# A recurrent two-tower network over 128 steps: path work less far ahead, the two column groups nearly a turn apart

## What is computed

```python
def _tower(x, w_in, b_in, blocks):          # _leaky(x) = where(x >= 0, x, 0.2 * x)
    h = _leaky(x @ w_in + b_in)
    for w1, b1, w2, b2 in blocks:           # two blocks, 128 x 128 each
        h = _leaky(_leaky(h @ w1 + b1) @ w2 + b2 + h)
    return h

def step(prev_delta, xk):
    fk, k = xk
    d = jnp.where(k == 0, fk[:, DELTA_IDX], prev_delta)
    fk = fk.at[:, DELTA_IDX].set(d)
    fe = _tower(fk[:, :4], fw_in, fb_in, flat_blocks)
    pe = _tower(fk[:, 4:], pw_in, pb_in, path_blocks)
    h = _leaky(jnp.concatenate([fe, pe], axis=-1) @ cw1 + cb1)
    delta = jax.nn.sigmoid(h @ cw2 + cb2)[:, 0]
    return (delta, delta)
```

## Time and profile before

| | |
|---|---|
| Median of 3 runs | 1250.41 us (1250.08 to 1253.89) |
| The profiled execution | 1254.54 us, its span 1252.7 us |
| PE busy | 1247.0 us, 6028 passes |
| PE weight loads busy | 1063.5 us |
| ACT busy | 931.0 us |
| DVE busy | 890.9 us |
| POOL busy | 11.8 us |
| DMA | 24.50 MB, 20 GB/s in the mean |

### The profile page before, as it was taken

One profiled execution on the slowest core, in us unless ns is written; L12 is line 12 of the kernel. 1 busy time (PEld: TensorE's weight loads), 2 busy tenths in 40 slices (PEclk: granted clock), 3 DMA queues, 4 the chain that ended last, 5 costly groups with the idle time before them and its releaser, 6 DMA issues.

```text
span 1252.7 us, 19624 instructions
## 1 busy us (share of the span) xinstructions
PE 1247.0 (100%) x6028; PEld 1063.5 (85%) x6028; DVE 890.9 (71%) x1950; ACT 931.0 (74%) x2049; POOL 11.8 (1%) x28
## 2 busy tenths in 40 slices
PE   9999999999999999999999999999999999999998
PEld 6888888888888888888888888888888888888886
DVE  3777777767777777777777777777777777777775
ACT  3777777777777777777777777777777777777776
POOL 1000000000000000000000000000000000000000
PEclk9999999999999999999999999999999999999999
DMA  2000000000000000001000000000000000000000
GB/s 75 30 10 31 13 10 30 13 30 10 24 20 11 29 13 24 17 10 33 11 23 19 12 30 10 30 13 11 29 14 29 10 21 22 11 23 12 13 4 1
DMA packets 14881, 24.50 MB, mean 20 GB/s; under 512 B 1983, under 2 KB 8214, under 8 KB 14782
## 3 DMA queue, kind: packets, MB, share of 16 engines
q1 hardware_dynamic: 13982, 22.33, 5.5%
q10 hardware_dynamic: 720, 0.66, 0.2%
q0 software_dynamic: 80, 0.26, 0.1%
HBM read 16.67 MB, written 6.55 MB: 19 GB/s over the span
## 4 chain that ended last, share of the span: by engine, by line
PE 98%; DMA 0%; ACT 0%; DVE 0%; issue 0%; ACTq 0%; DVEq 0%
PE ps_path L540 36%; PE ps_flat L540 18%; PE ps_res L543 18%; PE ps_head L670 9%; PE ps_head L665 9%; PE ps_head L683 2%; PE ps_head L678 2%; PE ps_path L570 2%; PE ps_flat L627 2%; DMA cb_col<-cb 0%; PE ps_path L565 0%; DVE f_t L448 0%; ACT delta L313 0%; DVE head_lo L482 0%; PE ps_flat L622 0%
## 5 line engine op out<-in xcount | busy, mean ns | idle before, releaser
L256 ACT ACTIVATE f_mid<-ps_flat,columns_sb 128x256 f32<-128x256 f32 x512 | 242.6, 474 | 161.9 <-PE ps_flat L540 155.5
L543 PE MATMUL ps_res<-f_mid,hidden_w 128*128 128x256 f32 x1024 | 306.1, 381 | 0.2
L540 PE MATMUL ps_path<-p_mid,hidden_w 128*128 128x256 f32 x1024 | 304.5, 380 | 0.0
L256 ACT ACTIVATE f_res<-ps_res 128x256 f32<-128x256 f32 x512 | 196.1, 384 | 62.4 <-PE ps_res L543 62.4
L540 PEld LDWEIGHTS ps_path<-p_mid,hidden_w 128*128 128x128 f32 x1024 | 190.9, 190 | 31.1 <-ACT p_mid L256 0.2
L543 PEld LDWEIGHTS ps_res<-f_mid,hidden_w 128*128 128x128 f32 x1024 | 168.6, 189 | 55.4 <-ACT f_mid L256 1.8
L414 DVE SCALAR_TENSOR_TENSOR p_sum<-ps_path,columns_sb,p_in 128x512 f32<-128x512 f32 x128 | 96.1, 751 | 126.9 <-PE ps_path L540 126.9
L256 ACT ACTIVATE p_mid<-ps_path,columns_sb 128x512 f32<-128x512 f32 x256 | 176.1, 688 | 6.4 <-PE ps_path L540 6.4
L476 DVE CAST head_hi<-head 128x256 fp32r<-128x256 f32 x256 | 75.3, 294 | 128.8 <-ACT head L256 128.7
L448 DVE SCALAR_TENSOR_TENSOR f_t<-delta,columns_sb,ps_flat 128x256 f32<-128x256 f32 x256 | 123.1, 481 | 50.0 <-ACT delta L313 48.9
L256 ACT ACTIVATE head<-ps_head,cb_scaled 128x256 f32<-128x256 f32 x256 | 121.2, 474 | 45.7 <-PE ps_head L670 39.6
(11 more groups left out here) (49 smaller groups left out, 1454.9 us busy)
## 6 DMA issues: line engine op xcount, KB each, us to landing
x_in<-x_hi SPq DMA_DIRECT2D x127, 48.0 KB
x_in<-x_lo SPq DMA_DIRECT2D x127, 48.0 KB
chunk_x<-x SPq DMA_DIRECT2D x16, 192.0 KB, 2.4
x_hi<-chunk_hi SPq DMA_DIRECT2D x16, 192.0 KB, 1.9
x_lo<-chunk_lo SPq DMA_DIRECT2D x16, 192.0 KB, 2.0
out<-delta SPq DMA_DIRECT2D x128, 2.0 KB
hidden_w<-hidden ACTq DMA_DIRECT2D x1, 384.0 KB, 5.7
hidden_w<-hidden ACTq DMA_DIRECT2D x1, 256.0 KB, 3.0
```

What stands on the lines that cost most here:

```text
L256: return act.activation(dst, src, ACT.Prelu, bias=bias, alpha=NEG)
L540: return pe.matmul(dst, weight[w_name], src, start=True, stop=True)
L543: return pe.matmul(dst, weight[w_name], src, start=False, stop=True, skip_group_check=True)
```

## The change

path_2b, the leaky function of the path's second sum, moves from DVE to ACT. The body of every engine is written anew and runs for k = 1 to 128. In body k the path work is now that of steps k (second half of path_2b), k + 1 and k + 2. Group 0 starts its step at the head of the body, and group 1 starts the same step about a third of the turn later and ends it (output_high, output_low, delta_out, head_high, head_low of k - 1) at the head of the next body. The openings are new lists: on DVE the input weights are split ahead of chunk 0, which now comes behind flat_delta and flat_in of both groups, and split_chunk(1) now stands ahead of path_2b_sum(0). In the lists of the openings only the new order is shown.

```diff
@@ -153,7 +153,7 @@
             return 0 <= k < STEPS
 
         def bodies(eng, body):
-            for k in range(FIRST_BODY, STEPS):
+            for k in range(FIRST_BODY, STEPS + 1):
                 body(k)
 
         @block.sync
@@ -276,6 +276,12 @@
                     act.wait_ge(s_p2a_mm, k + 1)
                     leaky(p_mid2[:, :], ps_path2[:, :], column["pr2_b1"]).then_inc(s_p2a_h, 1)
 
+            def path_2b(k):
+                par = k % 2
+                if exists(k):
+                    act.wait_ge(s_p2b_t, k + 1)
+                    leaky(p_res2[par][:, :], p_sum2[:, :]).then_inc(s_p2b_h, 1)
+
             def flat_1a(k, g):
                 if exists(k):
                     act.wait_ge(s_f1a_mm[g], k + 1)
@@ -315,49 +321,45 @@
 
             def body(k):
                 flat_1a(k, 0)
+                delta_out(k - 1, 1)
+                flat_1b(k, 0)
+                path_2b(k)
+                flat_2a(k, 0)
+                flat_1a(k, 1)
+                flat_2b(k, 0)
                 flat_1b(k, 1)
-                flat_1b(k, 0)
+                path_1b(k + 1)
+                head_out(k, 0)
                 flat_2a(k, 1)
-                flat_2a(k, 0)
+                path_in(k + 2)
                 flat_2b(k, 1)
-                path_1b(k + 2)
-                flat_2b(k, 0)
+                delta_out(k, 0)
+                path_2a(k + 1)
                 head_out(k, 1)
-                head_out(k, 0)
-                path_in(k + 3)
-                delta_out(k, 1)
-                path_2a(k + 2)
-                delta_out(k, 0)
-                path_1a(k + 3)
-                flat_1a(k + 1, 1)
+                path_1a(k + 2)
 
...
             path_in(0)
             path_1a(0)
             flat_1a(0, 0)
+            path_1b(0)
+            flat_1b(0, 0)
+            path_in(1)
             flat_1a(0, 1)
+            path_2a(0)
+            path_1a(1)
+            path_2b(0)
+            flat_2a(0, 0)
+            flat_2b(0, 0)
+            path_1b(1)
             flat_1b(0, 1)
+            head_out(0, 0)
             flat_2a(0, 1)
             path_in(2)
             flat_2b(0, 1)
+            delta_out(0, 0)
             path_2a(1)
             head_out(0, 1)
+            path_1a(2)
 
             bodies(act, body)
 
@@ -429,12 +431,6 @@
                         dve.wait_ge(s_p2b_h, k)
                     add(p_sum2[:, :], ps_path2[:, :], column["pr2_b2"], p_res1[par][:, :]).then_inc(s_p2b_t, 1)
 
-            def path_2b(k):
-                par = k % 2
-                if exists(k):
-                    dve.wait_ge(s_p2b_t, k + 1)
-                    leaky(p_res2[par][:, :], p_sum2[:, :]).then_inc(s_p2b_h, 1)
-
             def flat_delta(k, g):
                 par = k % 2
                 if exists(k):
@@ -490,46 +486,37 @@
             def body(k):
                 flat_delta(k, 0)
                 flat_in(k, 0)
+                head_high(k - 1, 1)
+                head_low(k - 1, 1)
+                flat_1b_old(k, 0)
+                path_2b_sum(k)
+                flat_delta(k, 1)
+                flat_in(k, 1)
+                flat_2b_old(k, 0)
                 flat_1b_old(k, 1)
-                flat_1b_old(k, 0)
-                path_1b_sum(k + 2)
+                path_1b_sum(k + 1)
                 flat_2b_old(k, 1)
-                flat_2b_old(k, 0)
-                path_2b_sum(k + 1)
-                path_2b(k + 1)
-                split_next_chunk(k)
-                head_high(k, 1)
-                head_low(k, 1)
                 head_high(k, 0)
                 head_low(k, 0)
-                flat_delta(k + 1, 1)
-                flat_in(k + 1, 1)
-
...
+                split_next_chunk(k)
+
             split_input_weights()
+            flat_delta(0, 1)
+            flat_in(0, 1)
             flat_delta(0, 0)
             flat_in(0, 0)
+            split_first_chunk()
+            flat_1b_old(0, 1)
             flat_1b_old(0, 0)
             path_1b_sum(0)
             flat_2b_old(0, 0)
+            split_chunk(1)
+            path_2b_sum(0)
             split_output_weights()
             path_1b_sum(1)
             head_high(0, 0)
+            flat_2b_old(0, 1)
             head_low(0, 0)
 
             bodies(dve, body)
 
@@ -685,32 +672,32 @@
 
             def body(k):
                 flat_1a(k, 0)
-                flat_1b(k, 1)
-                path_1b(k + 2, 1)
+                output_high(k - 1, 1)
+                path_2b(k, 1)
+                output_low(k - 1, 1)
+                flat_x(k, 1)
                 flat_1b(k, 0)
-                flat_2a(k, 1)
-                path_2b(k + 1, 1)
+                path_1b(k + 1, 0)
+                path_1b(k + 1, 1)
                 flat_2a(k, 0)
-                flat_2b(k, 1)
+                flat_1a(k, 1)
                 combine_path(k, 0)
                 flat_2b(k, 0)
+                flat_1b(k, 1)
+                combine_path(k, 1)
+                combine_flat(k, 0)
+                flat_2a(k, 1)
+                flat_x(k + 1, 0)
+                path_in(k + 2)
+                path_2a(k + 1, 0)
+                output_high(k, 0)
+                flat_2b(k, 1)
+                output_low(k, 0)
+                path_2a(k + 1, 1)
+                path_1a(k + 2, 0)
                 combine_flat(k, 1)
-                flat_x(k + 1, 0)
-                path_in(k + 3)
-                combine_flat(k, 0)
-                flat_x(k + 1, 1)
-                path_2a(k + 2, 0)
-                output_high(k, 1)
-                path_2a(k + 2, 1)
-                output_low(k, 1)
-                output_high(k, 0)
-                path_1a(k + 3, 0)
-                output_low(k, 0)
-                path_1a(k + 3, 1)
-                combine_path(k + 1, 1)
-                path_2b(k + 2, 0)
-                flat_1a(k + 1, 1)
-                path_1b(k + 3, 0)
+                path_1a(k + 2, 1)
+                path_2b(k + 1, 0)
 
             def output_weight_rows():
                 pe.wait_ge(s_one_row, 1)
@@ -724,58 +711,43 @@
...
                 if i >= WARM_UP - GROUPS:
                     opening.then_inc(s_res_open[i % GROUPS], 1)
             path_in(0)
+            flat_x(0, 1)
             flat_x(0, 0)
             path_1a(0, 0)
             path_1a(0, 1)
+            output_weight_rows()
             flat_1a(0, 0)
             path_1b(0, 0)
             path_1b(0, 1)
             flat_1a(0, 1)
             flat_1b(0, 0)
             path_in(1)
             path_2a(0, 0)
+            path_2a(0, 1)
             path_1a(1, 0)
             path_1a(1, 1)
+            path_2b(0, 0)
+            path_2b(0, 1)
             flat_2a(0, 0)
             path_1b(1, 0)
             path_1b(1, 1)
             flat_2b(0, 0)
+            combine_path(0, 0)
+            flat_1b(0, 1)
+            combine_flat(0, 0)
+            combine_path(0, 1)
+            flat_2a(0, 1)
+            path_2a(1, 0)
+            flat_x(1, 0)
             path_in(2)
+            output_high(0, 0)
             flat_2b(0, 1)
+            output_low(0, 0)
+            path_2a(1, 1)
             path_1a(2, 0)
+            combine_flat(0, 1)
             path_1a(2, 1)
             path_2b(1, 0)
 
             bodies(pe, body)
```

More of the change, by code:

```diff
@@ L336, in _ @@
             flat_1a(0, 0)
+            path_1b(0)
+            flat_1b(0, 0)
+            path_in(1)
             flat_1a(0, 1)
-            path_1b(0)
-            path_in(1)
+            path_2a(0)
[4 more added lines that the diff above has]
+            path_1b(1)
             flat_1b(0, 1)
-            flat_1b(0, 0)
-            path_1a(1)
-            path_2a(0)
+            head_out(0, 0)
             flat_2a(0, 1)
-            flat_2a(0, 0)
-            path_1b(1)
             path_in(2)
-            flat_2b(0, 0)
             flat_2b(0, 1)
-            path_1a(2)
+            delta_out(0, 0)
             path_2a(1)
             head_out(0, 1)
[L353 to L360, removed]
+            path_1a(2)
             bodies(act, body)
@@ L492, in body @@
                 flat_in(k, 0)
+                head_high(k - 1, 1)
[5 more added lines that the diff above has]
+                flat_2b_old(k, 0)
                 flat_1b_old(k, 1)
-                flat_1b_old(k, 0)
-                path_1b_sum(k + 2)
+                path_1b_sum(k + 1)
                 flat_2b_old(k, 1)
-                flat_2b_old(k, 0)
-                path_2b_sum(k + 1)
-                path_2b(k + 1)
-                split_next_chunk(k)
-                head_high(k, 1)
-                head_low(k, 1)
                 head_high(k, 0)
                 head_low(k, 0)
-                flat_delta(k + 1, 1)
-                flat_in(k + 1, 1)
-            split_first_chunk()
+                split_next_chunk(k)
             split_input_weights()
+            flat_delta(0, 1)
+            flat_in(0, 1)
             flat_delta(0, 0)
             flat_in(0, 0)
-            flat_delta(0, 1)
+            split_first_chunk()
```

(51 more changed lines are left out.)

## The result

The changed kernel takes 1272.93 us in the median of four runs (1271.49 to 1273.27) against 1252.15 for the kernel before beside it (1250.08 to 1253.97): a ratio of 1.0163, 95% interval 1.0145 to 1.0181. It is slower, by less than 2% but clear of the scatter: the slowest of these executions of before took 1253.97 us, the fastest of after 1271.49. The 1252.15 lies between two heaps of times of the kernel before (experiment 7), and none of the four took it. The profiled execution of after is 1272.63 us with a span of 1270.8, 18.1 above the one of before (1254.54, span 1252.7).

A forecast was written before the change was run, and what follows sets the result against it. It took PE's own work as the bound, so the middle could only gain holes; 9.5 (steps) + 4.8 (opening) + 3.2 (end) = +17.5 us on the 1250.4 median gave 1267.9, range 1256 to 1276.

The forecast's parts named there:

- opening: Up to flat_1a(1, 0): PE waits 7.3 us for late chunk 1, then runs at half clock; +4.8 us (+1.9 to +8.1).
- 125 steps: Steady steps run whole: 0.076 us a step of new PE holes, +9.5 us (bounds +6.2 and +12.5).
- end: From step 126 to the span's end, group 1 running behind group 0: +3.2 us.
- the residual decides: PE's flat_1b(k, 0) waits for DVE's flat_1b_old(k, 0): 0.070 us short, the larger of two shortfalls there.
- f_mid's hop: From flat_1a(k, 0) to flat_1b(k, 0): 0.789 us of products between, 0.833 wanted, 0.044 short.
- output_high(k, 0): On PE, waiting for the head: can start at 6.76 against its slot at 6.754, 0.006 us a step.
- The rival that the weight load doesn't wait for data: PE's weight loads: each hop 0.11 us shorter, both shortfalls gone, step stays 9.58, 1258.4 us; chance 10%.
- the one of more holes: Steady step: waits taken as met by 0.03 or less are not; 0.1 us a step more, 1280 us; chance 7%.
- lost to the clock: After the opening's hole, PE passes run at half speed for 5.9 us, losing 2.9 us.
- That the later group pays for it: End of the kernel: group 1's later finish pays for the opening's 5.4 us less work ahead of flat_1a(1, 0).
- The move of path_2b: Leaky function moved from DVE (0.69 us) to ACT (0.62), wanted by 3.2, ending at 2.8: costed at nothing.
- The step that was off is the last one: Forecast median: before's median, 1250.41, 4.1 us below its profiled execution, plus 17.5 gives 1267.9.

The follow-up runs named there:

- experiment 7: Kernel before with output_weight_rows on PE moved ahead of flat_1a(0, 0) in the opening; 1250.91 us median of 12 against 1251.02, ratio 0.9996.
- experiment 3: Changed kernel without head_low of group 1, without the bias of flat_1a in group 0, then without both; 1270.73, 1271.94 and 1267.6 us.
- experiment 1: Changed kernel with split_chunk(1) on DVE moved from the opening to the end of body 1; 1262.41 us, ratio to before 1.009.
- experiment 4: Changed kernel with DVE's split of chunk 0 back at the head of its opening list; 1271.43 us in one execution.
- experiment 5: Changed kernel with 36, then 46, unread bf16 products on PE filling the hole ahead of flat_2b(0, 0); 1272.3 and 1269.77 us.
- both cuts: Changed kernel without head_low of group 1 and without the bias of flat_1a in group 0; 1267.6 us, period 9.600.
- experiment 6: Changed kernel with path_2b put back from ACT on DVE, behind path_2b_sum; 1355.98 us in one execution, period 10.32.
- experiment 8: Changed kernel with split_chunk(1) at the end of body 1 and flat_1b_old(k, 0) between head_high and head_low on DVE; 1259.3 us, ratio to before 1.0053.
- experiment 2: Changed kernel with flat_1b_old(k, 0) ahead of head_high and head_low of (k - 1, 1) on DVE; 1282.79 us, ratio 1.0251.
- 36 products: Changed kernel with 36 unread bf16 products on PE between path_1b(1) and flat_2b(0, 0); 1272.3 us in one execution.
- 46 products: Changed kernel with 46 unread bf16 products on PE between path_1b(1) and flat_2b(0, 0); 1269.77 us in one execution.

## Why the prediction was right, and where it was off

The forecast was 17.5 us more, 1272.0 for the profiled execution and 1267.9 for the median. Measured were 18.1 more and 1272.63 for the one, 1272.93 for the other; by the two medians of four the change is 20.8. By the terms of the sum, from flat_1a(1, 0), flat_1a(126, 0) and the end of the span in the two profiles:

| term | forecast | measured | from |
|---|---|---|---|
| opening | +4.8 | +3.6 | 39.72 against 36.10 |
| 125 steps | +9.5 | +10.9 | 1208.8 against 1197.9 |
| end | +3.2 | +3.6 | 22.3 against 18.7 |

- **The steady step** went by its steps: the residual decides, f_mid's hop is second (experiment 3), output_high(k, 0) is the third. The chain 0.50, 0.40, 0.34, 0.48, 0.12 is in the rows of after to 0.01 as it was priced from the earlier trace rows. Forecast 0.076, measured 0.081 by the medians: 10.1 us. The other 0.8 are odd steps, below. The rival that the weight load doesn't wait for data fell: it starts 0.12 behind the residual, and the period is 9.66. So did the one of more holes.
- **The opening** went by its mechanism: chunk 0 later, chunk 1 at 28.2 (forecast 28.8), DVE idle for it 12.3 us, a hole ended at 31.1 (31.8), 2.4 us lost to the clock (2.9) (experiments 1, 4 and 5). These two make the 1.2 us between forecast and measurement: the transfer came 0.6 sooner than counted, and half speed lasted from 31.1 to about 35.8, not for 5.9 us. The 5.9 had been borrowed from the start, the nearest row there was, so that it came out near is partly luck. Mis-sized too is where the hole begins: 20.9 and not 24.5, 10.2 us and not 7.3, as the clock rose before 16 us in this execution. It did no harm and no good: the hole ends by the transfer.
- **The end**: step 126 took 9.50 as forecast, the last one and what follows 12.8 for 12.57. delta ended at 1268.67 + 0.47 = 1269.14, 11.15 behind flat_1a(127, 0) (forecast 10.97), and the span ended 1.7 later (1.6). That the later group pays for it is the prediction's account; no run tested it.
- **The move of path_2b** cost at most 0.018 us a step (experiment 3, both cuts), where it was put at nothing; without it the new order takes 10.32 (experiment 6).
- **The step that was off is the last one**, from the profiled execution to the median. I took the 4.1 us between the two for something that the kernel after would have as well, and subtracted it. By experiment 7 it is the early rise of the clock in the lower heap. The profile of after has the early rise already (20 passes for 16 to 21), and its hole ends by the transfer, at 31.1, whatever PE ran at before. So an early rise is spent in the hole, and the four executions of after make one heap, 1271.5 to 1273.3. A second reason isn't excluded: all eleven profiles of kernels in the new order have the early rise, and the four executions of experiment 8, where the hole is only 0.62 us, lie within 2.1 us. Perhaps the new opening never has the late one. Against the lower heap the change costs 22 us, against the upper one 18. The rows for it were there: three runs at 1250.1, 1250.4 and 1253.9, and a half-speed stretch up to 23.5 whose end decides 4 us.

## What to carry to other kernels

When PE has no hole, a new order can only be judged by laying every wait on a grid of the hops measured where PE really does wait; shortfalls of 0.04 and 0.07 us showed up to about a hundredth, 125 times over. An instruction whose data come late must not be queued ahead of one on the chain, least of all in an opening: moved behind, the same split of chunk 1 gave back 10.5 us. When a profile and the median differ, find what makes the difference before carrying it over to the kernel after: here it was an early clock, which the kernel after could gain nothing more from. And when an instruction is put forward in a tight queue, work out the new time of the one that it displaces (experiment 2).

## What the runs showed that was not expected

- The level that PE ran at in the first microseconds is not in the granted clock of most profiles: before and the kernel of experiment 7 both read 1.00 for 16 to 21 us, with 10 and 25 passes. In two of the thirteen (experiments 1 and 2: 0.50 and 0.56 for 10 to 15) it is. The fall after the hole is there, as 0.50. Count passes.
- A hole of 3.1 us, behind a PE that had been dense, was followed by passes 0.43 apart until 34.6 us (36 products). With no hole (46 products) and with one of 0.62 us (experiment 1) full speed stayed.
- On DVE the distance from start to start depends on what is read. Behind f_in (128x256) the residual of the other group starts 0.34 us later, and the residual that reads this f_in 0.46 later (before, and experiment 2). f_in starts 0.51 behind the f_t that it reads, head_lo 0.40 behind the shorter head_hi.
- A few steps in each profile are 0.1 to 0.4 us longer than the rest, mostly the same ones in different kernels (54 by 0.36, 25 by 0.13, 71 and 73 by 0.09 and 0.15). They sum to 0.3 us in before, 1.0 in after, 2.2 and 2.8 in experiments 1 and 4, 3.1 in the kernel of both cuts of experiment 3 and in experiment 8. That before has few may be because its waits have more room to take up a late instruction; this, and what makes one late, was not tried and stays open.
